# One core, residual GNN layer: TensorE's steps in two rolled loops, a shorter chain for the destination ids, 3 KB id packets, output stores after the last load

## The reference

```python
# x (6250,128), src/dst (200000,), edge_attr (200000,128), all f32 / int32; dst is sorted
agg = segment_sum(edge_attr, dst, num_segments=6250)       # (6250,128)
h   = concatenate([x, agg, u[batch]], axis=1)              # batch is all zeros: one row u[0]
h   = relu(h @ W1 + b1)
out = layernorm(x + h @ W2 + b2, axis=-1)                  # no scale or shift
```

## Time and profile before

| | |
|---|---|
| median of three runs | 297.55 us |
| profiled execution, its own time | 299.55 us |
| its span in the profile | 297.8 us |
| busy share PE / weight load / DVE / ACT / POOL | 72% / 56% / 55% / 16% / 14% |
| moved by DMA | 110.25 MB, mean 370 GB/s |
| queue q1 (SP) | 105.83 MB, 92.4% of 16 engines' span |
| queue q10 (ScalarE) | 4.00 MB, 4.1% |
| instruction queues q8 and q14 | 20 packets, 0.33 MB; 10 packets, 0.08 MB |
| chain that ended last | PE 66%, issue 19%, DMA 10%, DVE 3% |

### The profile page before, as it was taken

One profiled execution on the slowest core, in us unless ns is written; L12 is line 12 of the kernel. 1 busy time (PEld: TensorE's weight loads), 2 busy tenths in 40 slices (PEclk: granted clock), 3 DMA queues, 4 the chain that ended last, 5 costly groups with the idle time before them and its releaser, 6 DMA issues.

```text
span 297.8 us, 11309 instructions
## 1 busy us (share of the span) xinstructions
PE 214.3 (72%) x4996; PEld 166.4 (56%) x4996; DVE 162.7 (55%) x423; ACT 46.8 (16%) x98; POOL 42.6 (14%) x37
## 2 busy tenths in 40 slices
PE   0069966996999997676996676776566875965862
PEld 0067744674787865555865555565355564754651
DVE  7487434272578794654364833816534544484442
ACT  0121120120122221211210211112102012101110
POOL 8000010003003030300120300302003003003010
PEclk9998889796899999999598997989999697797995
DMA  7999999998999999999999999999999999999921
GB/s 186 378 359 400 401 383 346 316 371 320 375 365 404 406 401 405 404 399 405 400 399 406 400 401 410 400 404 406 400 407 405 399 410 403 396 406 398 395 88 47
DMA packets 39944, 110.25 MB, mean 370 GB/s; under 512 B 2453, under 2 KB 3626, under 8 KB 39914
## 3 DMA queue, kind: packets, MB, share of 16 engines
q1 hardware_dynamic: 36404, 105.83, 92.4%
q10 hardware_dynamic: 3510, 4.00, 4.1%
HBM read 106.63 MB, written 3.20 MB: 369 GB/s over the span
## 4 chain that ended last, share of the span: by engine, by line
PE 66%; issue 19%; DMA 10%; DVE 3%; ACTq 0%; POOL 0%; POOLq 0%; DVEq 0%
PE rows_ps L741 36%; PE cols_ps L754 16%; DMA slots<-in_edge_attr 6%; PE hid_ps L769 4%; DMA rest_int<-in_dst 3%; PE hid_ps L787 3%; PE hid_ps L778 3%; PE hid_ps L763 2%; DVE edge_node L519 1%; DVE low L502 1%; PE rows_ps L725 1%; PE hid_ps L870 0%; DVE z L610 0%; POOL rstd L351 0%; DVE dst_local L511 0%
## 5 line engine op out<-in xcount | busy, mean ns | idle before, releaser
L741 PE MATMUL rows_ps<-slots,hot 64*32 64x128 f32 (+1 forms) x4560 | 118.7, 297 | 58.0 <-issue 55.9
L741 PEld LDWEIGHTS rows_ps<-slots,hot 64*32 64x32 f32 (+1 forms) x4560 | 97.2, 116 | 80.7 <-issue 79.8
L573 DVE TENSOR_TENSOR agg_t<-agg_t,cols_ps 128x128 f32 (+1 forms) x65 | 21.7, 333 | 116.7 <-PE cols_ps L754 116.5
L553 DVE TENSOR_TENSOR hot<-edge_node,iota 128x768 f32<-128x768 f32 x65 | 62.7, 965 | 2.6 <-issue 1.6
L754 PE MATMUL cols_ps<-row_hot,rows 128*128 128x224 f32 (+1 forms) x190 | 54.2, 398 | 0.4 <-ACT rows L383 0.4
L351 POOL TENSOR_TENSOR rstd<-var_eps,minus_half 128x4 f32<-128x4 f32 (+1 forms) x13 | 19.9, 1533 | 221.6 <-DVE var_eps L604 221.6
L383 ACT ACTIVATE rows<-rows_ps 128x128 f32<-128x128 f32 (+1 forms) x65 | 21.2, 326 | 181.5 <-PE rows_ps L741 178.5
L754 PEld LDWEIGHTS cols_ps<-row_hot,rows 128*128 128x128 f32 x190 | 34.7, 212 | 16.0 <-issue 14.9
L342 POOL TENSOR_TENSOR z<-x_rows,b_all 128x512 f32<-128x512 f32 (+1 forms) x13 | 15.6, 1202 | 29.9 <-PE hid_ps L763 29.9
L610 DVE TENSOR_SCALAR z<-z,moments,rstd 128x128 f32<-128x128 f32 x49 | 18.2, 431 | 2.2 <-POOL rstd L351 2.0
L562 DVE TENSOR_TENSOR row_hot<-row_node,iota 128x448 f32<-128x448 f32 x30 | 18.5, 616 | 0.0
(11 more groups left out here) (100 smaller groups left out, 76.1 us busy)
## 6 DMA issues: line engine op xcount, KB each, us to landing
slots<-in_edge_attr SPq DMA_DIRECT2D x65, 1536.0 KB, 17.8
x_rows<-in_x ACTq DMA_DIRECT2D x11, 256.0 KB
out<-z SPq DMA_DIRECT2D x11, 256.0 KB
dst_int<-in_dst SPq DMA_DIRECT2D x1, 384.0 KB, 4.3
dst_int<-in_dst ACTq DMA_DIRECT2D x1, 384.0 KB, 6.0
x_rows<-in_x ACTq DMA_DIRECT2D x1, 192.0 KB
out<-z SPq DMA_DIRECT2D x1, 192.0 KB
rest_slot<-in_edge_attr ACTq DMA_DIRECT2D x1, 160.0 KB, 13.9
```

The costliest lines, as they stand in the source:

```text
L553: V.tensor_tensor(hot[i][:, :, :], edge_node[:, bass.ds(t, 1), :, :].rearrange("p o c r -> p (o c r)").unsqueeze(2).broadcast_to([P, RUNS, ...
L573: V.tensor_tensor(cols, cols, cols_ps[:, 0:n], ALU.add).then_inc(added, 1)
L741: done = T.matmul(rows_ps[i][c * SPAN:(c + 1) * SPAN, h, 0:feats], hot[j][part, c * RUN + r, :], slots[part, j, c, r * feats:(r + 1) * fea ...
```

## The change

TensorE's work becomes two loops, laps 0 to 5 (`sparse_lap`) and laps 6 to 12 (`dense_lap`), with the work of single laps under `pe.If`. Counters of semaphores get an offset (`rows_copied` by 2, `z_made` and `added` by 1), so that the same waits hold in the first lap. Level 1 of step 0 is now the loop's first step, and the products for the bias and the rest edges follow it. In a dense lap level 2 of step t directly follows level 1 of the same step, and the products and VectorE's work on the previous block come one step earlier. The ids are loaded as twice two transfers with 3 KB rows, `first_int` goes ahead of the loads on SP's queue, and `first_int` and `rest_int` have semaphores of their own. `low` is the first id of each window, not the minimum; the checks in `judge` get one more reduction and one more test. The base of each step comes from `low` by two operations on VectorE and three small products. GpSimd's clearing of `agg_t` is cut in 13 pieces. All stores stand behind the last load on SP.

```diff
+            for c in range(SHARE):
+                sp.dma_start(dst_int[0:held, HALVES * c:HALVES * (c + 1), :], dst_groups[0, c]).then_inc(dst_in, 16)
+            sp.dma_start(first_int[:, :, :], dst_first).then_inc(first_in, 16)
             for t in range(SLOTS, steps):
                 sp.wait_ge(level1_done, t - SLOTS + 1)
                 load(t)
-                if t % LAP == LAP - 1 and t // LAP >= 3:
-                    store(t // LAP - 3)
-            for i in range(laps - 3, final):
+            for i in range(final):
                 store(i)
...
-            G.memset(agg_t[:, :], 0.0).then_inc(agg_zero, 1)
+            for at in range(0, width, BLOCK):
+                done = G.memset(agg_t[:, at:min(at + BLOCK, width)], 0.0)
+            done.then_inc(agg_zero, 1)
...
-            dve.wait_ge(dst_in, 16 * 4)
-            then(V.tensor_reduce(low[:, :], dst_int[:, :, :], AX.X, ALU.min))
+            dve.wait_ge(dst_in, 16 * GROUPS * SHARE)
-            then(V.tensor_reduce(both[:, :], two, AX.X, ALU.min))
...
+            then(V.tensor_copy(low[:, :], dst_int[:, :, 0]))
+            then(V.tensor_tensor(fall[:, :], two[:, :, 0], two[:, :, 1], ALU.subtract))
+            then(V.scalar_tensor_tensor(two[:, :, 1], fall[:, :], dense[:, 0:1], two[:, :, 1], ALU.mult, ALU.add))
...
+            then(V.tensor_scalar(base[:, :], low[0:held, 0:1], 0.0, early[0:held, 0:1], ALU.max, ALU.mult))
+            dve.wait_ge(ident_made, 1)
+            V.tensor_scalar(base_diag[:, :], ident[0:held, 0:held], base[:, 0:1], None, ALU.mult).then_inc(base_made, 1)
...
+            dve.wait_ge(first_in, 16)
+            V.tensor_copy(edge_node[:, held, :, :], first_int[:, :, :])
             copy_ids(1)
+            dve.wait_ge(rest_ids_in, 16)
...
-            dve.wait_ge(least_turned, 1)
...
+                    k = j + 1 if lap >= DENSE_LAP else j
+                    if lap and k == 2:
                         residual(lap - 1, lap - 1)
+                    elif lap and k == 3:
                         variance(lap - 1, lap - 1)
-                        if lap == final:
-                            normalise(lap - 1, lap - 1)
+                    elif lap and k == 4:
                         normalise(lap - 1, lap - 1)
...
+            def sparse_lap(lap):
+                counts(lap)
                 for j in range(LAP):
                     t = lap * LAP + j
+                    level1(t, lap, j, False)
+                    if j:
+                        level2(t - 1, j - 1, False)
                     else:
+                        with pe.If(lap > 0):
+                            level2(t - 1, LAP - 1, False)
+                        with pe.If(lap < 1):
+                            first_products()
+                    if j == 1:
+                        with pe.If(lap > 0):
+                            finished(lap)
+                            product1_agg(lap - 1, start_of(lap - 1))
+                    elif j == 2:
+                        with pe.If(lap > 0):
+                            product2(lap - 1, lap - 1)
+                    elif j == 4:
+                        turn_x(lap, lap, lap * 16 + 16)
+            def dense_lap(lap):
...
+                    level1(t, lap, j, True)
...
+                    level2(t, j, True)
+            def first_products():
+                pe.wait_ge(w_in, 16 * weights)
...
+                pe.wait_ge(rest_in, 16)
+                pe.wait_ge(rest_hot_made, 1)
...
+            with pe.Fori(0, DENSE_LAP) as lap:
+                sparse_lap(lap)
+            level2(DENSE - 1, LAP - 1, False)
+            with pe.Fori(DENSE_LAP, laps) as lap:
+                dense_lap(lap)
+            pe.wait_ge(added, steps + 1)
+            product1_agg(final, start_of(final))
+            product2(final, final)
```

More of the change, by code:

```diff
@@ L135, in residual_gnn_layer @@
         dense = sb("dense", [P, 1])
-        both = sb("both", [P, SHARE])
-        fall = sb("fall", [P, SHARE * HALVES])
+        early = sb("early", [P, 1])
+        fall = sb("fall", [P, SHARE])
         end = sb("end", [P, 1])
@@ L433, in _ @@
                 copy_ids(k, False)
+            copy_rows(0)
             act.wait_ge(w_in, 16 * weights)
-            act.wait_ge(bias_done, 1)
-            A.activation(bias[:, :], hid_ps[:, 0:1], ACT.Identity, bias=b1_col[:, :]).then_inc(bias_made, 1)
             act.wait_ge(b2_done, 1)
+            A.activation(bias[:, :], bias_ps, ACT.Identity, bias=b1_col[:, :]).then_inc(bias_made, 1)
             A.activation(b2_all[:, :], b2_ps, ACT.Copy).then_inc(b2_made, 1)
             act.wait_ge(bias_made, 1)
[L441 to L459, removed]
+            for lap in range(laps):
+                dense_lap = lap >= DENSE_LAP
+                for j in range(LAP):
+                    t = lap * LAP + j
+                    if dense_lap:
+                        copy_rows(t)
+                    elif t + 1 < DENSE:
+                        copy_rows(t + 1)
+                    if j == 0 and lap:
+                        relu(lap - 1)
+                    elif j == 3:
+                        copy_x(lap)
+                    elif j == 4 and lap < final:
+                        load_x(lap + 1)
             relu(final)
@@ L567, in add @@
                 dve.wait_ge(level2_done, t + 1)
-                if not (isinstance(t, int) and t == 0):
-                    dve.wait_ge(added, t)
+                dve.wait_ge(added, t + 1)
                 n = DENSE_COLS if dense_step else COLS
@@ L758, in turn_x @@
                 pe.wait_ge(x_in, landed)
[L759 to L761 removed]
+                pe.wait_ge(z_made, seq + 1)
                 for r in range(rows_of(i)):
@@ new lines, in sparse_lap @@
+                    if j == 1:
[8 more added lines that the diff above has]
+            def dense_lap(lap):
+                counts(lap)
+                for j in range(LAP):
+                    t = lap * LAP + j
+                    if j == 4:
+                        with pe.If(lap > final - 1):
+                            product1_x(final, final)
+                    level1(t, lap, j, True)
+                    if j == 0:
+                        with pe.If(lap > final - 1):
+                            pe.wait_ge(bad_counted, 1)
+                            T.matmul(bad_ps, bad_count[:, :], ones[:, 0:1], start=True, stop=False)
+                            T.matmul(bad_ps, first_bad_count[:, :], ones[:, 0:1], start=False, stop=False)
+                            T.matmul(bad_ps, rest_bad_count[:, :], ones[0:HALF, 0:1], start=False, stop=True).then_inc(bad_summed, 1)
+                        finished(lap)
+                        with pe.If(lap < final):
+                            product1_agg(lap - 1, start_of(lap - 1))
+                        with pe.If(lap > final - 1):
+                            product1_agg(short, 0)
@@ new lines, in dense_lap @@
+                        with pe.If(lap < final):
+                            with pe.If(lap > short - 1):
+                                pe.wait_ge(x_in, x_landed(short))
+                            turn_x(lap, lap, lap * 16 + 16)
+                        with pe.If(lap > final - 1):
+                            turn_x(final, final, x_landed(final))
+                    level2(t, j, True)
+            def first_products():
+                pe.wait_ge(w_in, 16 * weights)
+                T.matmul(bias_ps, w1u[:, :], u_col[:, :], start=True, stop=True)
+                T.matmul(b2_ps, ones[0:1, :], b2_row[:, :], start=True, stop=True).then_inc(b2_done, 1)
+                pe.wait_ge(rest_in, 16)
+                pe.wait_ge(rest_hot_made, 1)
+                for r in range(rest_run):
+                    done = T.matmul(hid_ps[:, 0:SPAN], rest_slot[:, r * feats:(r + 1) * feats], rest_hot[:, r, :], start=(r == 0), stop=(r == rest_run - 1))
+                done.then_inc(rest_done, 1)
+                pe.wait_ge(row_node_made, 1)
+                pe.wait_ge(b2_made, 1)
```

156 lines of the change are left out of this document (41 added, 115 removed).

## The result

The changed kernel took 287.07 us in the median (286.12 to 288.01, four runs) against 296.73 us for the kernel before: a ratio of 0.9684 with a 95% interval of 0.961 to 0.9758. Timed again beside three of the experiments it took 286.38 us (285.77 to 286.64, six runs) against 297.51, ratio 0.9635 (0.9592 to 0.9677); this is the firmer figure, since the value 288.01 stands twice among the four above. The forecast was 284.8 us, in a range of 281 to 292, with 0.88 on faster. The direction, the mechanism and the range held; the gain of 9.7 to 11.1 us fell short of the 12.75 us of the sum.

What follows compares the result with a forecast made beforehand. DMA bytes were taken to set the pace, with TensorE late in the early slices. The span 297.8 - 5.85 - 6.4 - 1.2 + 0.7 = 285.05, then + 1.75 - 2.0, gave 284.8 us, range 281 to 292.

Steps and rivals of the forecast that it cites:

- the sum: Whole kernel: 297.8 - 5.85 - 6.4 - 1.2 + 0.7 = 285.05 us of span, giving 284.8 us as measured time.
- What bounds the kernel: DMA bytes set the pace from slice 13 at 395 to 410 GB/s; before that PE frees slots too late.
- Stores, -5.85: Nine 256 KB stores leave the stream ahead of the last load, which lands 5.85 us earlier at 403 GB/s.
- Starvation, -6.4: Rate dip in slices 6 to 12, from PE freeing slots late: an earlier start removes it, 6.4 us less.
- the first load, +0.7: Start of the loads: first load issued behind one more id transfer and `first_int`, taken as 0.7 us later.
- Its inner steps: Start: ids landed at 7.2, `dst_local` near 8.2, level 1 of step 1 at 20.5 us; together 10.3 us.
- Tail, -1.2: Last step: the add no longer waits behind `normalise` of the previous block, 1.2 us less (0.9 to 1.8).
- At nothing: Laps: ScalarE's copy exposed in dense laps, two more checks and the `If`s are covered and cost nothing.
- Rival 1: TensorE's loop jumps and skipping `If`s: code is fetched again on every turn, 42 us more, 327 us; chance 0.08.
- Rival 2: After the last load: 2.88 MB of writes outlast the last chain, +2.8 us at 220 GB/s, 287.6 us; chance 0.08.
- rival 3: Start: the ids come no earlier and perhaps half of the early starvation stays, 288 to 290 us; chance 0.13.
- rival 4: Id checks or TensorE's clock: the general path runs, or PE stays at low clock, 294 to 300 us; chance 0.04.

Runs made afterwards that it cites:

- before_stores_last: The kernel before with only the stores moved behind the last load: 292.15 us, ratio 0.9817 to the kernel before.
- unrolled: The changed kernel with all six sparse laps as code of their own, no loop: 295.47 us, ratio 0.9982 to the kernel before.
- zero_later: The changed kernel with GpSimd's clearing of `agg_t` put behind the subtraction of the ids: 286.30 us.
- late5: The changed kernel with five extra reductions, results unused, ahead of the first id operation: 289.26 us.
- stores_among: The changed kernel with the nine stores back among the loads: 290.98 us.
- nine_stores_less: The changed kernel without its first nine stores, the output of nine blocks left out: 286.63 us.

## Why the prediction was right or wrong, by its own steps

**What bounds the kernel: right.** Bytes set the pace, and the early dip was lateness of TensorE. In the changed kernel the rate is flat, and a delay of 7.0 us at the start came through with 3.0.

**Stores, -5.85: right in kind, too large.** 4.6 us from the changed kernel's side, 5.4 from the kernel's before. The sum priced the stores at the mixed rate, but gave the remaining reads the same rate; they run at 401, not 403. The sign named for it, a lap shorter by 0.65 us, came out as 0.5: 20.3 us in the changed kernel's second record (the turns of `x` at 73.56, 93.81, 114.16 and 134.42 us) against 20.8 (225.83, 246.59 and 267.39).

**Starvation, -6.4, and the first load, +0.7: the step that was mis-sized.** Up to the last level 1 they came to 4.6 us, not 5.7. The dip was gone altogether, but in `before_stores_last` it is only 77, 76, 20 and 130 GB/s in slices of 7.3 us, 5.5 us. I read 6.4 from one execution, which was itself 2.0 us above the median, and then took off these 2.0 us as well. That the excess sat in the dip, and so was counted twice, is argued from the two records, not shown. The loads' first issue moved from 1.44 to 2.98 us. Whether that cost the +0.7 can't be told: the first three slices of the changed kernel's second record (179, 373, 356) lack 36 GB/s against those of `before_stores_last` (197, 380, 367), some 0.6 us, but `unrolled`, which has the same start, has 180, 370 and 389.

**Its inner steps.** Ids landed at 6.7 (7.2 predicted) and the first operation began at once. It took 1.89 us where 0.2 was assumed, and ended at 8.65 us with GpSimd's clearings (8.62), of which cutting them in 13 was to free it. `zero_later` shows that they were the cause. But it was this operation alone that waited to their end: the five short ones from 2.68 to 3.47 us ran beside the clearings in 0.14 to 0.16 us each, and so did the reductions of `late5`. So `dst_local` began at 9.1, not 8.2. The new wait for `rest_slot` never showed: it landed at 7.0 + 8.8 = 15.8 us, not 19. Level 1 of step 1 began at 18.8 against 20.5; 1.2 us of this came from level 1 of step 0, which took 1.58 us where the steps had 2.77: luck, since the same product takes 2.82 us in `stores_among` and `unrolled`, whose start is the same. Of the 10.3 us "in hand" against 6.4, `late5` measured 4.0 as slack, nearly the difference.

**Tail, -1.2: right as to the order, partly hidden by the clock.** The add now follows level 2 at once, and at equal clock that gives 1.1 us (`stores_among` against `before_stores_last`), with 0.5 more behind it. But in the first record the last level 1 took 2.79 us at the lower clock (granted 0.50, 1.2 GHz) and the tail shrank by 0.7 us; in the second it took 1.62 us and the tail shrank by 2.1.

**At nothing: right.** The `If`s, the exposed copy and the checks left no mark on a flat rate.

**The sum.** Stores came out 1.25 us too large, starvation with the first load 1.1 us, and the tail 0.4 us too small (1.6 for 1.2): 1.9 us together, against the 1.6 us between 284.8 and 286.4. The mechanisms were right and these sizes off.

**Rival 1** did not come, but its mechanism exists. Code is kept for a loop of one lap and fetched again for one of two laps, at +18.7 us. The window of two pages that the Trainium skill ("Runtime: NRT & Kernel Launch", Instruction fetch mechanics) names would have made the changed loops fetch in every turn; they did not. The size that the same section of the Trainium skill gives for PE, 2,048 instructions, lies between the loop that stays (some 1,100) and the one that does not (some 2,200), and agrees. Its remark that kernels prefer full unrolling where possible does not hold here: unrolled laps cost 9.1 us. (The rival's price has a slip: 22.1 - 19.6 is 2.5 us for each of seven dense laps, not 2.) **Rival 2** is excluded by `nine_stores_less`, **rival 3** by the start's rows (15.24 us), **rival 4** by the span and the clock between 60 and 160 us (0.98 to 1.00). That rival took the 2.77 us of the first level 1 for the low clock; the granted clock reads 1.00 there, so this isn't shown.

## What to carry to other kernels

Where bytes set the pace, count which of them stand ahead of the last load, and put the rest under the last chain; then check at what rate what remains will run. What comes earlier than the slots' slack is worth nothing: measure the slack with one deliberate delay before shortening a start further. For TensorE's long code here the loop that stays loaded (some 1,100 instructions) was better than unrolled code, and the loop of twice the size was the worst of the three. Where between the two sizes the limit lies was not measured.

## What the runs showed of the hardware that was not expected

- A loop whose body is kept jumps without a gap; one of twice the size waited 5.36 and 5.50 us at its jumps, while new code in a straight line cost 9.1 us over 20 more packets, under 0.5 us each of the kernel's time.
- A 4-column copy on VectorE took 1.89 us beside GpSimd's run of 13 clearings, ending with it, and 0.17 us without it. Other operations beside the same clearings were hardly held or not at all: reductions of 1,536 columns took their 1.75 us, a copy of 24 columns 0.16 us. What decides which operation waits was not found.
- The last bytes come at 25 GB/s, a sixteenth of the full rate, for over 2 us from 274 us on, as if one of the 16 DMA engines were late. The last step starts only near the end of this. Whether it is always the same engine, and what makes it late, was not found.
- Reads mixed with writes ran at 403 GB/s, reads alone at 401.
